# The last tile of a fused AdaLN + FFN kernel: 384 and 128 columns in place of 256 and 256

## The reference, cut to what matters

```
h      = x mixed over channels                       # (64, 32, 512)
shared = relu(h @ up_w)**2 @ down_w                  # 512 -> 1024 -> 512
latent = h @ fc1_w                                   # 512 -> 256
moe    = (latent @ expert_w) * sum(top2(h @ gate_w)) # one scale per token
routed = moe @ fc2_w                                 # 256 -> 512
out    = x + layernorm(shared + routed) * gamma + beta   # over 512 features, eps 1e-5
```

## Time and profile before

| what | value |
|---|---|
| device time, median of 3 runs | 256.74 us (256.52 to 256.76) |
| profiled execution, span from the first to the last instruction | 254.6 us |
| PE busy | 248.0 us, 97% of the span |
| PEld busy | 207.1 us, 81% |
| DVE busy | 155.8 us, 61% |
| ACT busy | 81.8 us, 32% |
| POOL busy | 39.4 us, 15% |

### The profile page before, as it was taken

The page is one execution under the profiler, slowest core; times in us unless marked ns, Lnnn a source line. Parts: engine busy times, 40 slices in busy tenths (PEclk is TensorE's granted clock), DMA queues, the critical chain, the costliest instruction groups (busy, mean ns, idle before and its releaser), DMA issues.

```text
span 254.6 us, 3526 instructions
## 1 busy us (share of the span) xinstructions
PE 248.0 (97%) x1291; PEld 207.1 (81%) x1291; DVE 155.8 (61%) x272; ACT 81.8 (32%) x142; POOL 39.4 (15%) x45
## 2 busy tenths in 40 slices
PE   8999999999999999999999999999999999999992
PEld 7877887988888888888888888888888888788891
DVE  4798999944448964644447983464444953406453
ACT  4669856411003452321112534331111355202100
POOL 2400021000117120001114411001111700001110
PEclk9999999999999999999999999999999999999997
DMA  6994804001111400001111220000011100000111
GB/s 161 332 324 153 305 17 153 0 0 44 41 41 41 167 0 0 3 0 42 41 41 41 78 87 0 0 0 11 31 41 44 42 0 0 0 3 8 74 44 41
DMA packets 10444, 15.60 MB, mean 61 GB/s; under 512 B 1088, under 2 KB 4928, under 8 KB 10432
## 3 DMA queue, kind: packets, MB, share of 16 engines
q1 hardware_dynamic: 9984, 15.33, 17.6%
q10 hardware_dynamic: 448, 0.11, 0.2%
HBM read 11.23 MB, written 4.20 MB: 61 GB/s over the span
## 4 chain that ended last, share of the span: by engine, by line
PE 89%; DMA 3%; issue 2%; DVE 1%; SPq 1%; ACT 0%; POOL 0%; POOLq 0%; DVEq 0%
PE ps L932 27%; PE ps L934 27%; PE ps L933 27%; PE ps L906 4%; DMA late<-in_up_w_dram 3%; PE ps L998 2%; PE ps L950 1%; PE ps L956 1%; PE ps L952 1%; SPq L322 0%; POOL rstd L417 0%; DVE stats L714 0%; DVE y_buf L712 0%; DVE h_full L636 0%; ACT h_hi L474 0%
## 5 line engine op out<-in xcount | busy, mean ns | idle before, releaser
L932 PE MATMUL ps<-down_hi,sq_hi 128*128 128x512 f32 (+1 forms) x136 | 51.2, 377 | 0.0
L933 PE MATMUL ps<-down_lo,sq_hi 128*128 128x512 f32 (+1 forms) x136 | 51.2, 377 | 0.0
L934 PE MATMUL ps<-down_hi,sq_lo 128*128 128x512 f32 (+1 forms) x136 | 51.2, 376 | 0.0
L932 PE MATMUL ps<-h_hi,up_hi 128*128 128x512 f32 x120 | 46.8, 390 | 0.0
L934 PE MATMUL ps<-h_hi,up_lo 128*128 128x512 f32 x120 | 46.7, 389 | 0.0
L933 PE MATMUL ps<-h_lo,up_hi 128*128 128x512 f32 x120 | 46.7, 389 | 0.0
L417 POOL TENSOR_TENSOR rstd<-mv,half 128x1 f32<-128x1 f32 x16 | 15.3, 954 | 158.2 <-DVE mv L719 153.2
L512 ACT ACTIVATE relu_sq<-ps 128x512 f32<-128x512 f32 x32 | 19.1, 597 | 57.7 <-PE ps L934 44.3
L712 DVE TENSOR_TENSOR y_buf<-ps,y_buf 128x512 f32<-128x512 f32 x15 | 10.4, 692 | 41.0 <-PE ps L934 40.7
L685 DVE CAST sq_hi<-relu_sq 128x512 fp32r<-128x512 f32 x32 | 22.6, 706 | 16.2 <-ACT relu_sq L514 15.7
L932 PEld LDWEIGHTS ps<-down_hi,sq_hi 128*128 128x128 f32 x136 | 25.6, 188 | 4.7
(11 more groups left out here) (137 smaller groups left out, 308.7 us busy)
## 6 DMA issues: line engine op xcount, KB each, us to landing
out_dram<-late SPq DMA_DIRECT2D x15, 256.0 KB, 2.0
x_cur<-in_x_dram SPq DMA_DIRECT2D x3, 1024.0 KB, 5.2
late<-in_down_w_dram SPq DMA_DIRECT2D x4, 512.0 KB, 5.3
late<-in_up_w_dram SPq DMA_DIRECT2D x3, 512.0 KB, 8.8
x_cur<-in_x_dram SPq DMA_DIRECT2D x2, 512.0 KB, 7.2
experts_sb<-in_experts_dram SPq DMA_DIRECT2D x3, 256.0 KB, 3.5
agg_b<-aggb_dram SPq DMA_DIRECT2D x1, 768.0 KB, 4.9
latents_sb<-in_latents_dram SPq DMA_DIRECT2D x1, 528.0 KB, 4.8
```

What stands on the lines that cost most here:

```text
L932: nc.tensor.matmul(dst, a_hi, b_hi, start=first, stop=False)
L933: nc.tensor.matmul(dst, a_hi, b_lo, start=False, stop=False)
L934: return nc.tensor.matmul(dst, a_lo, b_hi, start=False, stop=last)
```

## The change

The last tile's columns are cut at 384 in place of 256. Everything else about the two parts stays: their banks, the order of the matmuls, the semaphores, the order on DVE and SP.

```diff
-        def last_shared(half):
-
-            return [shared(TB - 1), ps[:, LAT_BANK[0], :]][half][:, 0:HID // 2]
+        LAST_COLS = [slice(0, 3 * HID // 4), slice(3 * HID // 4, HID)]
+
+        def last_shared(part):
+
+            width = LAST_COLS[part].stop - LAST_COLS[part].start
+            return [shared(TB - 1), ps[:, LAT_BANK[0], :]][part][:, 0:width]
...
-            for half in (0, 1):
-                cols = slice(half * HID // 2, (half + 1) * HID // 2)
-                sp.wait_ge(final_done, NT + half)
+            for part, cols in enumerate(LAST_COLS):
+                sp.wait_ge(final_done, NT + part)
                 sp.dma_start(out_v[:, NT - 1:NT, cols], out_buf[:, TB - 1:TB, cols]).then_inc(stored[TB - 1], 16)
...
-                halves = [slice(0, HID // 2), slice(HID // 2, HID)]
-                for i, cols in enumerate(halves):
+                for i, cols in enumerate(LAST_COLS):
                     dve.wait_ge(shared_done, n + i)
                     nc.vector.bn_stats(out=last_stats[:, i, :], in_=last_shared(i)).then_inc(stats_done, 1)
...
-                        for half in (0, 1):
-                            cols = slice(half * HID // 2, (half + 1) * HID // 2)
+                        for part, cols in enumerate(LAST_COLS):
                             for lc in range(LC):
-                                three_products(last_shared(half), lat_hi[:, lc, rows], lat_lo[:, lc, rows],
+                                three_products(last_shared(part), lat_hi[:, lc, rows], lat_lo[:, lc, rows],
                                                q_hi[:, lc, cols], q_lo[:, lc, cols], lc == 0, False)
```

More of the change, by code:

```diff
@@ L755, in normalise_last @@
                 dve.wait_ge(stored[t], 16 * b)
-                for cols in halves:
+                for cols in LAST_COLS:
                     nc.vector.scalar_tensor_tensor(out=out_buf[:, t, cols], in0=y[:, cols], scalar=rstd[:, :],
@@ L1012, in down_product @@
                         pe.wait_ge(last_lo_ready, LC)
-                        for half in (0, 1):
-                            cols = slice(half * HID // 2, (half + 1) * HID // 2)
+                        for part, cols in enumerate(LAST_COLS):
                             for lc in range(LC):
-                                three_products(last_shared(half), lat_hi[:, lc, rows], lat_lo[:, lc, rows],
+                                three_products(last_shared(part), lat_hi[:, lc, rows], lat_lo[:, lc, rows],
                                                q_hi[:, lc, cols], q_lo[:, lc, cols], lc == 0, False)
                             for m in range(IC):
-                                last = three_products(last_shared(half), sq_hi[:, m, rows], sq_lo[:, m, rows],
+                                last = three_products(last_shared(part), sq_hi[:, m, rows], sq_lo[:, m, rows],
                                                       down_hi[:, m, cols], down_lo[:, m, cols],
```

## The result

The changed kernel takes 257.6 us (median of 5 runs, 257.32 to 258.02) against 256.57 us before (256.35 to 256.76). The ratio is 1.0049, 95% interval 1.0038 to 1.0059: 1.26 us slower by the ratio, 1.0 to 1.5 by its interval (the two medians lie 1.03 us apart). The forecast was 258.15 us, 1.42 us slower, with 256.5 to 258.7 as its range.

The account below looks back on a forecast made before the run. PE's stream of matmuls, busy 97% of the span, was taken as the bound, with everything from the last matmul on one chain. The terms summed to 29c - 2058 ns, +1.42 us at c = 120, giving 258.15 us, range 256.5 to 258.7.

Parts of the forecast that it names:

- The wide part pays in full: Last tile's 384-column part on PE: matmuls 173.2 ns apart, interpolated between 119.8 at 256 columns and 226.7 at 512.
- The narrow part waits for its weight load: Last tile's 128-column part on PE: a full 128-column load, priced at 105 to 120 ns, sets the matmuls' pace.
- c = 120 ns: c is the pace of part 1's 128-column matmuls in the last tile; taken as 120 ns, bounds 66 and 240.
- 29c - 1872: Change in ns of the last matmul's start behind the last tile's first; +1.61 us with c at 120 ns.
- The cut at 256 sat where stream and load are equal: Old last tile's two 256-column parts: a full load hides exactly behind a stream of 120 ns.
- The last matmul's length: Last tile's final matmul on PE: about 230 ns at 128 columns against 283 at 256, -0.05 us.
- bn_stats at 128 columns: Part 1's bn_stats behind the last matmul: 297 ns against 430 at 256 columns, -0.13 us.
- The pairs: Paired instructions at L749 and L757 in the tail: about 612 and 350 ns, span still 0.88 us, no change.
- The stores: Two final output stores, 192 and 64 KB: taken as no change, with bounds of 0.2 us either way.
- Stream alone: Rival for part 1 on PE: loads run ahead, matmuls 66 ns apart, -0.13 us, 256.6 us; chance 0.14.
- In between: Rival for part 1 on PE: matmuls 70 to 89 ns apart, same within what can be told, 257.0 us; chance 0.10.
- Like fp32: Rival for part 1: narrow f32r matmuls run like plain fp32, 240 ns per product, +4.90 us, 261.6 us; chance 0.16.

Follow-up runs that it names:

- w288_224: Last tile cut at 288 and 224 columns, against the kernel before with 256 and 256; ratio 1.0001 (0.9992 to 1.0010).
- load64: Changed kernel, but part 1 loads only the first 64 of the tile's 128 tokens as stationary operand; ratio 0.9989 to the kernel before.
- load96: Changed kernel, but part 1 loads only the first 96 of the tile's 128 tokens as stationary operand; ratio 1.0027 to the kernel before.

## Why the prediction was right, and what was mis-sized

- **PE is the bound and only the tail moves.** Right. Everything in front of the last tile took as long as before, apart from the prologue's 0.34 us, which is in the execution and not in the change.
- **The wide part pays in full.** Right: 173.2 ns forecast, 174 measured; 132, 146 and 203 ns at 288, 320 and 448 columns lie within 3 ns of the same line.
- **The narrow part waits for its weight load.** Right, and now shown from both sides: 109, 111 and 111 ns at 64, 192 and 224 columns with a full load, and 110, 84 and 60 ns at 128 columns with 128, 96 and 64 columns of load.
- **c = 120 ns.** This term was mis-sized: 110 ns, within the 105 to 120 that the rows allowed. With it 29c - 1872 gives 1.32 us, measured 1.34; I had 1.61. I took 120 from two rows that, read by their starts, give less. These are lines of the kernel before (x31 is the mixing's stretch of 32 without its first record):

```profile
10.42 0.13 PEld L902 LDWEIGHTS ps<-bias_sb,att_T 8*64 8x64 f32 x1
43.97 3.84 PE L906 MATMUL ps<-mix,x_cur 128*128 128x128 f32 x32
44.18 3.62 PE L906 MATMUL ps<-mix,x_cur 128*128 128x128 f32 x31
6.89 1.03 PE L859 MATMUL ps<-experts_sb 128*128 128x256 f32 x4
```

The second load of L902 starts 10.42 - 10.37 = 0.05 us behind the first; the 0.06 was a difference of rounded lengths. Doubled, 0.05 to 0.06 us is 100 to 120 ns, and L881's 0.055 is 110. The mixing's 120 ns was busy time over count, which holds the whole length of a stretch's last record and a slow first interval (43.97 to 44.18); behind these its records start (3.62 - 0.28)/30 = 111 ns apart. That is the pace of part 1, but it does not prove a load either: the plain fp32 records of 256 columns start (1.03 - 0.38)/3 = 217 ns apart, which would make some 108 ns of stream for 128 columns. The slope of the load records (105 ns) came close as well.
- **The cut at 256 sat where stream and load are equal.** Nearly: the stream's 120 ns is 8 ns over the load's 112, and in w288_224 the last matmul starts only 0.1 us later than before.
- **The last matmul's length**: forecast 230 ns by the line through 389 and 283, measured 275. It gives 0.01 us back in place of 0.05. With a load of 64 columns, in load64, its group shows 223 ns, close to the line, so the load lengthens it:

```profile
L935 PE MATMUL ps<-down_hi,sq_lo 128*64 128x128 f32 x8 | 1.5, 223 | 0.0
```

- **bn_stats at 128 columns**: 297 ns forecast, 0.30 us measured, -0.13 us. **The pairs**: nothing, right. **The stores**: nothing, right within 0.05 us.
- Together the terms measure 1.34 - 0.01 - 0.13 = 1.20 us, where the forecast had 1.42. The traces from the tile's first matmul to the end (1.2 us) and the ratio (1.26 us) agree. The miss of 0.22 us is the 0.29 us of c, less some 0.07 us by which part 0 and the last matmul took longer than forecast.
- **The rivals.** Stream alone fell, since c is 110 ns and not 66. In between fell; the Trainium skill's 81 ns for a 128-column pair ("TensorE: Matmul & The Clock Gate", section "Back-to-back issue gap") does not hold for these 4-byte operands with a full load, where four widths show 109 to 111 ns. Like fp32 (240 ns) fell too. The Trainium skill's load time (same page, section "LDWEIGHTS (loading the stationary operand)"), 107 ns for 128 columns, lies 3 ns under the measured mean and 5 under the 112 from the second matmul on; the 1.05 us worked out from it was an estimate, 0.15 us under the 1.20 measured.

## What to carry to other kernels

Find the weight load's own time before cutting a matmul's moving side. Here matmuls with 128 columns of load in f32r start 110 to 112 ns apart at the least, so they are free to shrink only down to about 235 moving columns (an estimate: the width at which 13 ns plus 0.418 ns per column make 110 to 112 ns); below that, each column moved to the wide part costs its stream there and gives nothing back. And price a cut with all its sides: it doubles the loads, and what it hides (a bn_stats of 0.43 us) may be no more than what its extra matmuls cost (30 x 13 ns and the rest).

## What the runs showed of the hardware that I had not expected

The extra over the bare stream is not a constant of the matmul. With a full load it is 12 to 16 ns at 256 to 512 columns (13 in the kernel before); with 64 columns of load it is 6.7 ns at 256 (113.4 - 106.7) and 6.4 ns at 128 (59.7 - 53.3), and with 32 columns of load it is still 6.7 (60.0 - 53.3). Why it is about twice as large with a full load, and where it changes between 64 and 128 columns of load, stays open: load96 cannot show it, since its 84 ns are the load's.

The first of a row of narrow matmuls escapes the load. In part 1 of the changed kernel the second starts 0.06 us behind the first, close to the stream's pace, and only from the third on are they 0.11 us apart; with 64 columns the first interval is 0.03 us. It may be that the load for it ran beside the wide matmul in front, but that is argued and not shown: the record of this load starts at 247.84 us, with the first narrow matmul.

Every matmul of these traces has a load of its own (1291 and 1291), also the first two of each three, which use the same stationary operand (q_hi and q_lo with lat_hi). What a kernel would gain without the second of these loads was not tried.
